# A nine-tap convolution from five products per three outputs instead of four per two, with a new order of its parts

## The reference, cut to what matters

```
y = conv1d_same(x, sh_w1, sh_b1)      # 128 -> 512 channels, 9 taps, over 748 rows
y = silu(y)
y = conv1d_same(y, sh_w2, sh_b2)      # 512 -> 128 channels, 1 tap
# added to the routed experts' sum; layer norm (ln_g, ln_b) and the residual follow
```

## Time and profile before

| what | value |
|---|---|
| median of 3 runs | 1534.27 us (1530.68 to 1536.31) |
| the profiled execution's own time | 1544.43 us |
| its span, first to last instruction | 1542.6 us |
| PE busy | 1305.9 us, 85% of the span |
| DVE busy | 1003.6 us, 65% |
| POOL busy | 699.3 us, 45% |
| ACT busy | 644.9 us, 42% |
| mean granted TensorE clock | 0.92 |

### The profile page before, as it was taken

One profiled execution on the slowest core, in us unless ns is written; L12 is line 12 of the kernel. 1 busy time (PEld: TensorE's weight loads), 2 busy tenths in 40 slices (PEclk: granted clock), 3 DMA queues, 4 the chain that ended last, 5 costly groups with the idle time before them and its releaser, 6 DMA issues.

```text
span 1542.6 us, 33397 instructions
## 1 busy us (share of the span) xinstructions
PE 1305.9 (85%) x10360; PEld 1103.2 (72%) x10361; DVE 1003.6 (65%) x3235; ACT 644.9 (42%) x1610; POOL 699.3 (45%) x1055
## 2 busy tenths in 40 slices
PE   6696777787899937778899899988998989999974
PEld 3464646564899935556788778876887989999953
DVE  4467768665466656757863786467663628989946
ACT  1346272523122204335335453445334436666623
POOL 0112556444688853133531444242614526777732
PEclk9697989898999978989999899999998999999987
DMA  6000400003588840010010001000100237777725
GB/s 191 4 21 6 111 27 22 25 21 95 161 266 256 263 170 1 2 42 1 24 61 0 2 14 58 14 1 1 43 1 8 95 97 191 196 194 198 196 88 161
DMA packets 102202, 128.46 MB, mean 83 GB/s; under 512 B 21015, under 2 KB 61181, under 8 KB 101842
## 3 DMA queue, kind: packets, MB, share of 16 engines
q1 hardware_dynamic: 88786, 102.36, 23.1%
q0 software_dynamic: 13312, 24.74, 4.8%
HBM read 96.13 MB, written 34.94 MB: 85 GB/s over the span
## 4 chain that ended last, share of the span: by engine, by line
PE 60%; DVE 15%; issue 7%; DVEq 6%; POOL 5%; ACT 4%; DMA 2%; POOLq 0%; SPq 0%; ACTq 0%
PE psum L980 12%; PE psum L1133 11%; PE psum L989 9%; DVE work L1554 3%; PE psum L1142 3%; PE psum L1047 2%; POOL rows_in L2130 2%; PE psum L1094 2%; PE psum L1072 2%; PE psum L794 2%; PE psum L1191 2%; PE psum L969 2%; PE psum L1018 2%; DVE stats L1537 2%; PE psum L1067 1%
## 5 line engine op out<-in xcount | busy, mean ns | idle before, releaser
L1133 PE MATMUL psum<-NT,wreg 128*128 128x182 f32 (+1 forms) x1536 | 261.6, 326 | 10.2 <-ACT pack L1434 5.1
L1133 PEld LDWEIGHTS psum<-NT,wreg 128*128 128x128 f32 x1536 | 247.9, 192 | 18.9 <-ACT pack L1434 5.9
L2162 POOL DMA_INDIRECT rows_out<-work,expert_row_kept x208 | 206.2, 992 | 79.6 <-issue 41.1
L980 PE MATMUL psum<-work 128*128 128x128 f32 x1664 | 222.7, 277 | 0.9 <-ACT work L1336 0.9
L980 PEld LDWEIGHTS psum<-work 128*128 128x128 f32 x1664 | 203.9, 193 | 1.7 <-issue 0.9
L2111 POOL TENSOR_TENSOR rstd<-var_eps,pack 128x6 f32<-128x6 f32 x40 | 56.5, 1415 | 215.0 <-DVE var_eps L1544 214.9
L1329 ACT ACTIVATE work<-psum,work 128x128 f32<-128x128 f32 x416 | 118.6, 368 | 64.4 <-PE psum L980 64.3
L1876 DVE SCALAR_TENSOR_TENSOR work<-psum,work 128x128 f32<-128x128 f32 x416 | 117.1, 344 | 7.7
L794 PE MATMUL psum<-pack,work 128*128 128x128 f32 (+2 forms) x288 | 51.4, 336 | 82.0 <-DVE work L1554 75.5
L1885 DVE TENSOR_SCALAR work<-psum,expert_row_kept 128x128 f32<-128x128 f32 x208 | 72.8, 350 | 71.8 <-PE psum L969 36.6
L2130 POOL DMA_INDIRECT rows_in<-N,slot_now x96 | 100.5, 1046 | 28.6 <-issue 28.4
(11 more groups left out here) (364 smaller groups left out, 2894.3 us busy)
## 6 DMA issues: line engine op xcount, KB each, us to landing
work<-w_and_b SPq DMA_DIRECT2D x104, 258.0 KB
work<-in_ew SPq DMA_DIRECT2D x104, 256.0 KB
work<-rows_in SPq DMA_DIRECT2D x208, 65.0 KB
work<-rows_out SPq DMA_DIRECT2D x32, 384.0 KB, 4.2
rows_out<-work,expert_row_kept POOLq DMA_INDIRECT x208
work<-in_xT SPq DMA_DIRECT2D x8, 375.0 KB, 3.0
w_and_b<-in_ew SPq DMA_DIRECT2D x1, 2560.0 KB
out<-H SPq DMA_DIRECT2D x8, 320.0 KB
```

The costliest lines, as they stand in the source:

```text
L980: r_ = mm(v.ps1[:, c * P:(c + 1) * P], v.w1[:, c * P:(c + 1) * P], v.xT, start=True, stop=True)
L1133: r = mm(bank[:, half * HALF_PAIRS:half * HALF_PAIRS + p1 - p0], weights[:, m * P:(m + 1) * P], product_input(name, g, k, p0, p1), start=( ...
L2162: G.indirect_dma_start(rows_out[m], bass.IndirectOffsetOnAxis(ap=v.dest, axis=0), v.y, None, bounds_check=last, oob_is_err=False).then_inc ...
```

## The change

Three outputs now come from five products, over triples of outputs. A product has 250 columns (`TRIPLES`) and covers all 748 rows of a lane, so there are 8 units (k, m) in an iteration instead of 16. A unit has three parts: `p12` (products 1 and 2, six matmuls), `p03` (six) and `p4` (three). DVE combines a unit in seven operations of 250 columns. POOL's `turn` has 12 operations of 252 columns (one of them twice that), in four groups with drains between; `make_conv_weights` has eight operations of 1536 columns in place of three. The Silu works on 748 columns at once. The second convolution's `rows` 0 and 1 stand together in the middle of an iteration, `rows` 2 and 3 together at its end.

In POOL's queue `turn` of lane 1 moves from the start of the next iteration to the end of its own. The addition of `ln_b` becomes `add_ln_b`, ahead of it. `rows` 0 and 1 move behind `rstd6`, `rows` 2 behind `add_b_sh2` of lane 0.

Two of the four buffers of hidden rows now lie in the first 12 tiles of `H`. These tiles are stored to DRAM once, after iteration 0, and loaded back at the end of `experts1`. The weights come in by four DMAs instead of two. In iteration 0 alone, from step 2 to the chunks, lane 1's steps stand one step behind lane 0's.

```diff
+TRIPLES = (L + 2) // 3
+TURNED = TRIPLES + 2
...
-        conv_h = sb("conv_h", [P, 4, SPAN[0][1]])
...
+        conv_h = [conv_h_own[:, m, :] for m in range(2)] + [
+            H[:, m * TILES:(m + 1) * TILES, :].rearrange("p j d -> p (j d)") for m in range(2)]
...
-        UNIT = [(q, m) for q in range(UNITS) for m in range(4)]
+        UNIT = [(k, m) for k in range(LANES) for m in range(4)]
+        POINTS = {"p12": (1, 2), "p03": (0, 3), "p4": (4,)}
...
+        for k, m in UNIT:
+            PARTS.append(("p12", k, m))
+            if m == 1 and k > 0:
+                PARTS += [("rows", 2 * k - 2, 0), ("rows", 2 * k - 1, 0)]
+            PARTS += [("p03", k, m), ("p4", k, m)]
+        CONV_END = [("last", LANES - 1, 3), ("rows", UNITS - 2, 0), ("rows", UNITS - 1, 0)]
+        COST = {"p12": 6, "p03": 6, "p4": 3, "rows": 4}
...
-        FILL = [3, 1, 0, 0, 0, 0, 1, 0] + [0.5, 0.5] * TILES + [3.5, 2, 1.5, 1, 0.5]
+        FILL = [3, 1, 0, 0, 0, 0, 1, 0] + [0.5, 0.5] * TILES + [3.5, 2.5, 2, 1, 0]
...
+            if not conv:
+                ahead = [x for x in turns_ if x[0] < CHUNKS]
+                ahead.sort(key=lambda x: (x[0] + (x[1] if x[0] > 1 else 0), x[1]))
+                turns_ = ahead + turns_[len(ahead):]
...
+                while conv and n < len(PARTS) and sum(costs[:n]) * sum(FILL) * LANES < reached * sum(costs):
...
+            sp.wait_ge(first_rows_final, 1)
+            sp.dma_start(first_rows_dram, first_rows).then_inc(first_rows_out, 16)
...
+            sp.dma_start(first_rows, first_rows_dram).then_inc(first_rows_back, 16)
...
+                    for half, x in enumerate(POINTS[what]):
                         for g in range(3):
+                            r = mm(bank[:, half * TRIPLES:(half + 1) * TRIPLES], conv_w[:, x, g, k_cols(m)], turned(k)[:, x, g:g + TRIPLES],
+                                   start=(g == 0), stop=(g == 2))
...
+                if k > 0 and in_first(i):
+                    norm5(k, i)
...
-                V.tensor_tensor(conv_sum[:, 0:n_], b, c, ALU.add)
-                V.tensor_tensor(b, b, c, ALU.subtract)
+                V.scalar_tensor_tensor(conv_sum, p1, 3.0, p2, ALU.mult, ALU.add)
+                V.scalar_tensor_tensor(p2, p1, -3.0, p2, ALU.mult, ALU.add)
+                V.scalar_tensor_tensor(p0, p0, 3.0, p3, ALU.mult, ALU.add)
+                V.scalar_tensor_tensor(conv_p4, conv_p4, 1.5, p3, ALU.mult, ALU.add)
                 e.drain()
-                V.scalar_tensor_tensor(y[:, 0], conv_sum[:, 0:n_], 0.5, a, ALU.mult, ALU.add)
-                V.scalar_tensor_tensor(y[:, 1], b, 0.5, d_, ALU.mult, ALU.subtract
+                V.tensor_tensor(y[:, 0], p0, conv_sum, ALU.subtract)
+                V.scalar_tensor_tensor(y[:, 1], p3, 2.0, p2, ALU.mult, ALU.add)
+                V.scalar_tensor_tensor(y[:, 2], conv_p4, 4.0, conv_sum, ALU.mult, ALU.subtract
...
+                G.tensor_tensor(s, w0, w4, ALU.add)
+                G.tensor_tensor(w3, w1, w1, ALU.add)
                 e.drain()
+                G.tensor_tensor(w2, s, w1, ALU.subtract)
+                G.tensor_tensor(w3, w3, w0, ALU.add)
                 e.drain()
+                G.tensor_tensor(w1, w1, s, ALU.add)
+                e.drain()
+                G.tensor_tensor(s, w4, w4, ALU.add)
+                e.drain()
+                G.tensor_tensor(s, s, s, ALU.add)
+                e.drain()
+                G.tensor_tensor(w3, w3, s, ALU.add)
+                e.drain().then_inc(conv_made, 1)
...
+                e.wait_ge(pe_conv_done, pe_conv.at("conv", f"p43_{k}", 0, i - 1))
...
+                G.tensor_tensor(t[:, 3:5], x(3, 2), x(1, 2), ALU.subtract)
+                G.tensor_tensor(t[:, 0], x(0), x(2), ALU.subtract)
+                G.tensor_tensor(t[:, 1], x(1), x(2), ALU.add)
+                G.tensor_tensor(t[:, 2], x(1), x(2), ALU.subtract)
+                e.drain()
...
             def attention(i, first):
-                if not first:
-                    turn(1, i - 1)
...
                 for k in range(LANES):
                     rstd("attention", 6, k, i)
                 if not first:
-                    add_conv_rows(2, i - 1)
+                    add_conv_rows(0, i - 1)
+                    add_conv_rows(1, i - 1)
                 turn(0, i)
+                for k in range(LANES):
+                    add_ln_b(k, i, first)
+                turn(1, i)
                 add_b_sh2(0, i)
                 if not first:
+                    add_conv_rows(2, i - 1)
                     add_conv_rows(3, i - 1)
```

More of the change, by code:

```diff
@@ L564, in audio_tower, with fill_bank, fill_before, unit_before @@
         pool_conv_done = sem("pool_conv_done")
         pool_conv = Steps({"conv": (ITERS, 1, [f"rows{q}" for q in range(UNITS)])})
[L567 to L569 removed]
+        def fill_bank(name):
+            return conv_bank[FILLS.index(name) % 2]
+        def fill_before(name, i):
+            f = FILLS.index(name) - 2
+            return FILLS[f], (i if f >= 0 else i - 1)
+        def unit_before(k, m, i, back=1):
+            u = 4 * k + m - back
+            return (*UNIT[u], i if u >= 0 else i - 1)
```

254 lines of the change are left out of this document (133 added, 121 removed).

## The result

The changed kernel takes 1556.94 us (median of 4 runs, 1554.77 to 1565.2) where the kernel before, on the same chip, takes 1532.6 us (4 runs): ratio 1.0164, 95% interval 1.0111 to 1.0217. It is slower by 24 us, clear of the noise; 1511 with a range of 1488 to 1532 was forecast. The profiled execution took 1565.2 us, its span is 1563.1 us and its mean clock 0.896.

A forecast was written before the change was run, and what follows sets the result against it. PE was taken to set the pace of iterations 1 to 3, the chain between engines that of iteration 0. Terms +13, -12.2, twice -8.2, -8 and +0.5 gave -23.1 from 1534.3: 1511 us, range 1488 to 1532.

The forecast's parts named there:

- Columns: PE's products: 240 records take 50.7 us, which frees 12 us in each of three iterations and the tail.
- Iteration 0: First iteration grows by 13 us: +15 as POOL's five more weight operations stop DVE, -2 from the lanes' stagger.
- (D): Rival: the stagger in iteration 0 brings nothing, as PE waits for ACT; 1513 us, chance counted in the forecast's 0.66.
- PE's wait at the seam: Between iterations, PE's wait for the last combination and Silu grows by 2.5 us, bounds +1 and +5.3.
- Start of the next iteration: From the last combination's end to lane 1's norm on PE: 24 us in place of 26, -2 us.
- Iteration 1's start: Lane 1's norm comes some 20 us after the start instead of 25.7, with `turn` begun earlier: -6 us.
- Between the seams: From lane 1's norm to the next scores, 85% of 10.2 us of PE work is gained: -8.7 us per iteration.
- The tail: From the last iteration's end to the first expert matmul: 78.9 us for 87.0, -8 us, at best -12.
- The rest: Storing and reloading 12 tiles of `H` and the four weight DMAs are off the path; +0.5 in the sum.
- (B): Rival: the chain sets the loop once filler is taken out; 1 us back between the seams, 1534 us, chance 0.14.
- (C): Rival: POOL's longer `turn` stops DVE at the combinations, 13.6 us more per iteration; 1553 us, chance 0.08.
- (A): Rival: all of PE's columns are on the path, POOL's weights fall beside it; -48.5, 1486 us, chance 0.12.

The follow-up runs named there:

- run 1: Changed kernel with three of POOL's eight weight operations in iteration 0: 1648.13 us beside 1656.78 for the kernel before, ratio 0.9949.
- run 8: Changed kernel with the weights made by five DVE operations beside iteration 0's projections, none by POOL: 1550.41 us, ratio 1.0104 to the kernel before.
- run 10: Changed kernel with unit 0's combination moved behind lane 1's norm: 1653.11 us beside 1652.39 for the kernel before, ratio 0.9991.
- run 4: Changed kernel with two of the three matmul groups of every product: 1520.52 us beside 1532.93 for the kernel before, ratio 0.9927.
- run 3: Kernel before with five sixths of the columns in its products: ratios 0.9888, 0.9893 and 0.9877 to the unedited kernel before, in three sessions.
- run 2: Changed kernel with four operations in DVE's combination instead of seven: 1646.16 us beside 1656.78 for the kernel before, ratio 0.9929.
- run 6: Changed kernel with POOL's `turn` cut to its first group, 5 of 12 operations: 1653.37 us beside 1652.73 for the kernel before, ratio 1.0009.
- run 5: Changed kernel with a fourth matmul group in each product, the third one again: 1701.18 us beside 1652.73 for the kernel before, ratio 1.0306.
- run 7: Changed kernel with two of the four matmuls in each tile of `rows`: 1645.81 us beside 1652.73 for the kernel before, ratio 0.9952.
- 13: The last version: 12 with the last unit's combination and Silu ahead of lane 0's scores: 1643.21 us beside 1665.25; short session 1521.71 beside 1533.47 (kernel before).
- 12: Changed kernel with parts reordered, weights on DVE and twelve one-column POOL additions in their place: 1643.09 us, ratio 0.9932 to the kernel before.
- 9: Run 8 with the convolution's end ahead of the scores and filler moved: 1549.11 us, ratio 1.0101 to the kernel before.

## Why the prediction was wrong

- **Columns.** "240 records, 50.7 us": 51.37 in the tail. Right.
- **Iteration 0**, +13: +7.5 (124.02 for 116.54). The weights' five added operations cost 8.0, not 15 (run 1). I took 3 us each from one stretch of two operations; all three together cost some 3.4 (56.6 us of chunks before; 53.2 in run 8, with none on POOL). Three of the eight take 2.74 us, and of the 15 us that POOL works longer 7 do not show in the time; the bound of their full duration (+17) was not near. These are the rows:

```profile
609.52 3.47 POOL L2258 TENSOR_TENSOR N<-wreg 128x1536 f32<-128x1536 f32 x1
...
611.57 4.40 DVE L1987 SCALAR_TENSOR_TENSOR first_row<-pack,psum,first_row 128x64 f32<-128x64 f32 x2
612.95 2.74 POOL L2259 TENSOR_TENSOR wreg<-wreg 128x1536 f32<-128x1536 f32 x1
...
617.72 2.04 PE L1081 MATMUL psum<-work 64*128 64x256 f32 x8 [4.76 <-DVE work L1994]
```

  The stagger brought nothing: the first chunk starts 31.9 us into the iteration, 32.0 before. (D) held there.
- **PE's wait at the seam**, +2.5: +2.9. Right in mechanism and size.
- **Start of the next iteration**, 24 us: 27.0. This step failed. Up to lane 0's norm the chain was even 1 us early (+14.0 for +15.2). Then the combination of unit 0 was put down at 4 us and took 6.3 (to +20.3), because it waits for records of PE that start only behind ACT's copy of the second `rows`; and lane 1's variance, `rstd5` and norm took 6.7 for 5, the norm alone 2.98 us beside an addition of POOL. Run 10 moved this combination alone and took 4 to 5 us off two of the three seams. Iteration 1's start gave 2.7 of the 6 us (lane 1's norm 23.0 us behind it, 25.7 before).
- **Between the seams**, -8.7: +1.6, +2.9 and +0.1 us in iterations 1 to 3, from the first projection to the scores. This is the step that failed most, 10 us an iteration. "I count 85%" of the columns there; in the new order they were worth 0.53 of their time (run 4), and 0.45 in the old one, measured in long sessions alone (run 3). I read "PE's waits between the seams are short" as PE being the bound. Short waits show that filler fitted the gaps of the chain, not that the chain was shorter. By parts, in iterations 2 and 3: the queries grow by 1.7 us, as 18 records of products stand there instead of 12 (4.1 for 2.0 us). The chunks have 5 to 6 us less of PE's work and change by +0.8 and -1.9. The end has 5.8 us less of products (156 records, 26.3 us; 96 of 214 ns, 20.5) and grows by 0.3. There one can see it happen. Iteration 3 before:

```profile
1128.02 1.60 PE L1086 MATMUL psum<-pack,work 128*128 128x128 f32 x12
...
1146.38 0.86 PE L794 MATMUL psum<-pack,work 128*128 128x128 f32 x6 [0.15 <-DVE work L1554]
```

  and after:

```profile
1150.22 1.60 PE L1120 MATMUL psum<-pack,work 128*128 128x128 f32 x12 [0.96 <-DVE work L1994]
...
1168.78 1.51 PE L828 MATMUL psum<-pack,work 128*128 128x128 f32 x6 [3.95 <-DVE work L1587]
1170.08 6.00 PE L1175 MATMUL psum<-NT,wreg 128*128 128x250 f32 x18
...
1182.88 3.96 PE L1175 MATMUL psum<-NT,wreg 128*128 128x250 f32 x18
```

  Lane 0's second norm reaches PE 18.4 us behind the first output matmul before, 18.6 after, in each of iterations 1 to 3. PE had just enough filler for this time; with less it waits 3.95 us, and the clock falls behind the wait: 18 records take 6.00 us where later ones take 3.96, the norm's transposes 1.51 for 0.86. The waits (3.8 us more) and the clock (2.7) eat all that the columns freed in the end. With DVE's combination of four operations (run 2) the norm comes at 17.1 us and the wait is 2.5, so 1.5 us of it are the three added operations; these cost 3.5 us in a whole iteration. Over the whole stretch the clock fell from 0.96 to 0.93; of the 10.2 us that should have left PE, 7.2 did.
- **The tail**, -8: -5.7 (81.25 for 86.95). The work of PE was right (72.9 us; the terms sum to 72.6), the waits were not: 8.4 us for 6.3. A wait of 1.6 us for ACT's copy of `conv_p` was put at nothing. The last `rows` stand behind a wait of 4.97 us (4.5) and take 8.0 us (8.1):

```profile
1277.86 1.19 PE L1168 MATMUL psum<-wreg,conv_h 128*128 128x128 f32 x4 [4.97 <-ACT H L1455]
...
1286.90 0.41 PE L1003 MATMUL psum<-pack,work 128*128 128x128 f32 x2 [0.82 <-ACT conv_rows L1473]
```

- **The rest**, +0.5: +1.2, and 3.8 us in the first part of the program, where nothing was changed (574.28 for 570.50; in the traces of the short sessions it is 559 to 574).

The profiled sum is 7.5 + 2.4 + 7.3 + 4.1 - 5.7 + 1.2 + 3.8 = 20.6 us (1563.1 - 1542.6 = 20.5), the forecast was -23.1; 42 of the 44 us between them are the three iterations. (B) had the mechanism nearest, the chain sets the loop, but let it come out even: it lacked the chain's own growth. (C) named a time close to the result, 1553, but by luck: run 6 refutes its mechanism. (A) falls with runs 3 to 5.

Shown: the seam's parts (runs 7, 10, 13), the weights (1, 8, 12), the worth of columns in the new order (4, 5), and in the end the norm's time, PE's wait and the clock (the rows above, run 2). Argued only: how the loss splits in the chunks, where PE's waits for the mask and the context rose. Not tried: fewer columns in the old order where chunks take 67 us, so that 0.45 may not hold there.

## What to carry to other kernels

When an engine is 92% busy with filler beside a latency chain, price the filler by an experiment that takes some of it away, before trading it for work on the chain's engines: here a microsecond of PE's filler was worth half of one, and one of DVE's (run 2), or of `rows` (run 7), at the seam was worth a whole one. Look for the place where filler just fits the time up to a norm: what is taken from it comes back as a wait, and the clock falls behind it. A change that halves the number of stages (four units of rows to two) moves more work to the last stage; look for what then stands between the last result and the loop's turn, and place it anew on every in-order queue. Of the 35 us that the last version won back some 12 are the weights, moved to DVE, and the other 23 the order; its products and combinations are those of the changed kernel.

## What the runs showed of the hardware

**A pause of POOL.** Once in iteration 0, in every trace of the case, POOL stands still for 8.6 us with nothing awaited, behind 845 of its records (850 in runs 8 and 9), whatever instruction follows. What it is was not shown; in runs 12 and 13 twelve tiny instructions took the place of the weights, and the pause fell among them.

**The turn of the loop.** From pass to pass of the loop (iterations 1 to 3) DVE starts 3.0 us after its last instruction of the one before (1014.06 to 1017.10 before, 1034.98 to 1038.05 after, with 3.03 us in the last run), so what stands last on DVE is followed by these 3 us. Iteration 0 stands ahead of the loop, and behind it there is no such gap. In each gap of the six traces looked at a DMA packet of instructions (8192 bytes) starts 1.0 to 1.4 us after it begins (at 1015.2 before, 1036.2 after); whether DVE waits for it is not shown.

**Two kinds of session.** In some sessions both kernels take 120 us longer, with the chunks of iterations 1 to 3 at 87 to 91 us; the part ahead of iteration 0 takes 592 to 612 us where it takes 559 to 574 in short ones. Whether this belongs to the chip is open: all runs known to be of chip 2 were short, all of chips 1, 5, 8 and 13 long, and for the first result the chip is not on record. The same chunks of the changed kernel in a short session and in a long one:

```profile
912.72:979.55 66.83, 57.86 (x777) 44.58 (x777) 47.91 (x119) 22.94 (x61) 29.23 (x35) 0.92 0.09 28
```

```profile
975.10:1065.00 89.90, 66.65 (x777) 48.43 (x777) 48.01 (x119) 22.94 (x61) 28.98 (x35) 0.85 0.07 21
```

DVE, ACT and POOL are busy as long as before. PE has waits of about 1 us in which nothing is awaited, between matmuls of one kind, and the clock falls with them (view of waits, long session):

```profile
PE psum L1101 <- issue: 8.6, 9, 1.7
PE psum L1101 <- DVE work L1967: 5.4, 2, 4.7
PE psum L1106 <- issue: 4.8, 8, 1.0
```

In the short session the two "issue" rows are absent. The chunks are where POOL issues its indirect transfers one after another; iteration 0, which has none, is as long in either session (124.0 and 123.9 us). The cause stays open. The DMA packets of instructions give no hint: seven in the stretch, of 1.18 us each in the mean, in either trace. In such a session work beside the chunks is nearly free (run 5's 5 us more of columns there leave the chunks at 90.8 to 91.4 us, 89.6 to 91.1 in the changed kernel), and a change of it can't be judged.
